# Eleven row gathers of an edge slot issued in rows of three, the later rows held for TensorE's progress (graph convolutions, one core)

## What is computed

```
def conv(h, W, b):
    m = jnp.concatenate([h[dst], h[src], edge_attr], axis=1) @ W + b
    return jax.ops.segment_sum(m, dst, num_segments=n_nodes)
h = jax.nn.relu(conv(x, W1, b1))
h = jax.nn.relu(conv(h, W2, b2))
return conv(h, W3, b3)
```

## Time and profile before

| what | us |
|---|---|
| median of 3 runs | 12742.13 |
| lowest, highest | 12732.27, 12769.19 |
| span of the profiled execution | 13058.8 |
| POOL busy in it | 5588.0 |
| PE busy in it | 8138.5 |
| convolutions 1, 2, 3, roughly | 82 to 2458, 2466 to 4150, 4150 to 5890 |

### The profile page before, as it was taken

The page is one execution under the profiler, slowest core; times in us unless marked ns, Lnnn a source line. Parts: engine busy times, 40 slices in busy tenths (PEclk is TensorE's granted clock), DMA queues, the critical chain, the costliest instruction groups (busy, mean ns, idle before and its releaser), DMA issues. The chain is left out here.

```text
span 13058.8 us, 166557 instructions
## 1 busy us (share of the span) xinstructions
PE 8138.5 (62%) x53406; PEld 6241.7 (48%) x53407; DVE 4466.3 (34%) x5989; ACT 2268.9 (17%) x3783; POOL 5588.0 (43%) x5903
## 2 busy tenths in 40 slices
PE   5676667666666666665565665565655555555565
PEld 3444444455555555554444444444444444444444
DVE  5444444211112111113333333333443333333334
ACT  4444444100000000001111111111111111111112
POOL 3333332444443444443444444444344444444443
PEclk8877888777776776776777777777777777777777
DMA  4333334344445444443111111111111111111111
GB/s 144 143 136 142 138 139 142 133 164 164 164 164 168 165 164 164 164 164 89 42 42 42 45 41 45 42 38 42 42 57 41 42 42 42 44 41 39 42 43 53
DMA packets 409727, 1226.47 MB, mean 94 GB/s; under 512 B 119675, under 2 KB 212947, under 8 KB 360990
## 3 DMA queue, kind: packets, MB, share of 16 engines
q1 hardware_dynamic: 207943, 741.50, 15.8%
q0 software_dynamic: 188528, 235.73, 7.8%
q10 hardware_dynamic: 13160, 248.08, 4.8%
HBM read 943.27 MB, written 281.57 MB: 94 GB/s over the span
## 5 line engine op out<-in xcount | busy, mean ns | idle before, releaser
L2095 POOL DMA_INDIRECT data<-q_rows,idx x3328 | 3159.9, 949 | 3809.6 <-ACT idx L2223 2722.0
L971 POOL DMA_INDIRECT data<-h_parts,idx x2508 | 2382.6, 950 | 3422.0 <-PE p_part L986 2505.3
L1101 PE MATMUL p_z<-hs,adj 128*128 128x192 bf16 x22442 | 2779.3, 276 | 1291.2 <-issue 1277.0
L1101 PEld LDWEIGHTS p_z<-hs,adj 128*128 128x128 bf16 x22442 | 2189.8, 109 | 1981.3 <-issue 1799.9
L2299 DVE TENSOR_TENSOR_SCAN run<-reset,run,p_turn 128x1024 f32<-128x1024 bf16 x416 | 976.3, 2347 | 2841.3 <-DMA nodes<-kept_quads 2407.5
L2126 PE MATMUL part<-hot,back 128*128 128x128 f32 x6688 | 1069.2, 315 | 738.0 <-ACT back L2228 387.1
L2115 PE MATMUL p_back<-ident,run 128*128 128x128 f32 x3344 | 596.9, 338 | 1250.3 <-DVE run L2299 1206.8
L2126 PEld LDWEIGHTS part<-hot,back 128*128 128x128 f32 x6688 | 973.9, 226 | 736.6 <-issue 736.0
L2228 ACT COPY back<-p_back 128x1024 f32<-128x1024 f32 x418 | 423.2, 1012 | 5115.9 <-PE p_back L2115 3092.3
L2115 PEld LDWEIGHTS p_back<-ident,run 128*128 128x128 f32 x3344 | 509.5, 179 | 1632.7 <-issue 1632.6
L2121 PE MATMUL part<-hot,t 128*128 128x128 f32 x6688 | 1036.4, 321 | 254.8 <-issue 254.4
(11 more groups left out here) (363 smaller groups left out, 6537.6 us busy)
## 6 DMA issues: line engine op xcount, KB each, us to landing
adj<-counted SPq DMA_DIRECT2D x304, 1568.0 KB
counted<-adj ACTq DMA_DIRECT2D x76, 3136.0 KB
reset<-flags SPq DMA_DIRECT2D x208, 512.0 KB
data<-q_rows,idx POOLq DMA_INDIRECT x3328
data<-h_parts,idx POOLq DMA_INDIRECT x2508
feat<-in_ea_blocks SPq DMA_DIRECT2D x208, 128.0 KB
ea<-in_ea_cols SPq DMA_DIRECT2D x154, 88.0 KB, 1.9
rden<-node_rows SPq DMA_DIRECT2D x50, 256.0 KB
```

The lines of the kernel that those rows point to most:

```text
L971: pool.indirect_dma_start(out=data[:, p % HELD, j, 0:PARTS], out_offset=None, in_=table[:, :], in_offset=bass.IndirectOffsetOnAxis(ap=idx[ ...
L1101: mm = pe.matmul(p_z[:, 0:PARTS], adj[:, (q + LAG) % 2, hi, :], hs[:, hi, :], start=(hi == 0), stop=(hi == BLOCKS - 1))
L2095: pool.indirect_dma_start(out=data[:, r, j, :], out_offset=None, in_=q_rows[:, :], in_offset=bass.IndirectOffsetOnAxis(ap=idx[:, r, j:j + ...
```

## The change

POOL's eleven gathers of a slot are cut into rows of 3, 3, 3 and 2. The first row goes out as before; ahead of columns 3, 6 and 9 POOL waits for TensorE's progress through the dense group that follows the `by_window` that freed the slot. In convolutions 2 and 3 the marks are the blocks `hi` 32, 64 and 80, for which PE's matmuls get a new semaphore `s_pace`; in convolution 1 they are the ends of count steps 2, 5 and 8 (the semaphore `s_count`, which was there). At the start, slots that have no such dense group yet (`alone`) are gathered without the waits, and for this the first turn of POOL's loop stands outside of it.

```diff
+    PACED = (3, 6, 9)
+    PACES = (32, 64, 80)
...
+        s_pace = sem("s_pace")
...
-            with pool.Fori(0, KT) as k:
+            def paced(k, p, j):
+
+                group = k * NQ + (p + 1 - HELD)
+                if first:
+                    pool.wait_ge(s_count, group * GC + (j + 2))
+                else:
+                    pool.wait_ge(s_pace, group * (len(PACES)) + PACED.index(j) + 1)
+                gate(pool)
+
+            def gather(k, p, pos, alone):
+                pool.wait_ge(s_idx[p], k + 1)
+                pool.wait_ge(s_part, k * H + (H + nth[pos] + 1 - HELD * (H // len(POS_P))))
+                gate(pool)
+                for j in range(GC):
+                    if j in PACED and not alone:
+                        paced(k, p, j)
+                    pool.indirect_dma_start(
+                        out=data[:, p % HELD, j, 0:PARTS], out_offset=None, in_=table[:, :],
+                        in_offset=bass.IndirectOffsetOnAxis(ap=idx[:, p, j:j + 1], axis=0),
+                    ).then_inc(s_row[p], 16)
+
+            for p, pos in enumerate(POS_P):
+                gather(0, p, pos, p + 1 < HELD)
+            with pool.Fori(1, KT) as k:
                 for p, pos in enumerate(POS_P):
-                    pool.wait_ge(s_idx[p], k + 1)
...
+                    gather(k, p, pos, False)
...
+                        if not first and hi in PACES:
+                            mm.then_inc(s_pace, 1)
```

More of the change, by code:

```diff
@@ L964, in _ @@
             further_windows_of(pool, further)
-            with pool.Fori(0, KT) as k:
-                for p, pos in enumerate(POS_P):
-                    pool.wait_ge(s_idx[p], k + 1)
[L968 to L974, removed]
+            def paced(k, p, j):
[19 more added lines that the diff above has]
+            with pool.Fori(1, KT) as k:
+                for p, pos in enumerate(POS_P):
+                    gather(k, p, pos, False)
         @block.tensor
```

## The result

The changed kernel takes 11967.9 us (median of 3 runs, 11958.6 to 11972.0), the kernel before 12742.1: a ratio of 0.939, with a 95% interval of 0.937 to 0.941. The forecast was 11960 us. The profiled run of the changed kernel is its timed run, so here span and time agree.

The account below looks back on a forecast made before the run. No engine was taken as full; POOL's gather bursts were taken to slow TensorE and hold up its semaphores. Convolutions 2 and 3 -433, convolution 1 -395, waits +50 made -778 us: 11960 us, range 11300 to 12850.

Parts of the forecast that it names:

- The cause: In the convolutions, POOL's gather burst slows TensorE after some 55 to 60 pairs and holds its semaphores; 8.7 us a slot.
- Rival 1: Convolutions: the burst is not the cause, nothing gained, only the waits' cost remains; 12790 us, chance 0.07.
- The rule of the Trainium skill: At SBUF, TensorE never waits on anyone, so gathers do not slow PE; no saving, only 50 us of waits.
- Row 1, then row 2: Convolutions 2 and 3: block 32's wait holds nothing, six gathers form one 7.5 us burst, PE slows at 5.0 us.
- Rows 3 and 4: Convolutions 2 and 3: block 64's wait pauses POOL 3.0 us; then five gathers follow directly, 6.25 us.
- Convolutions 2 and 3, the sum: POOL binds with one and a half pauses, 18.25 us a slot against 21.1; 433 us less.
- Convolution 1, the sum: Burst ends 6.0 us earlier, the work behind it stays; 22.5 us a slot, 395 us less.
- The waits: POOL's satisfied waits cost 0.1 us each on the 456 of convolutions 2 and 3; 50 us more.
- The sum: Whole kernel: -433 - 395 + 50 = -778 us; 11964 us against the median, stated as 11960.
- Rival 2: At the group's boundary, rows 3 and 4 hold PE's semaphores until row 4 ends; slower, 13150 us, chance 0.13.
- Rival 3: Convolutions: more gained, one pause a slot at 16.75 us, convolution 1 at 18.5 us; 11380 us, chance 0.2.
- What would show it: Trace signs: gathers in six and five, 17 to 20 and 20 to 24 us slots, PE's "issue" time about halved.

Follow-up runs that it names:

- g_timed: The change, but in convolutions 2 and 3 one 1700-element memset between third and fourth gather replaces the waits; 12020.5 us, 0.920 of the kernel before.
- g_timed2: The change, but in convolutions 2 and 3 one 700-element memset between third and fourth gather replaces the waits; 11878.3 us, 0.928 of the kernel before (chip B).
- e_before: The kernel before, unchanged, run again for a second trace; 13087.9 us, ratio 1.000, profiled span 13097 us.
- c_onewait: The change, but in convolutions 2 and 3 only the wait for block 32 is kept; 12132.9 us, 0.928 of the kernel before.
- r_after: The change, unchanged, run beside the kernel before on one chip; 12114.9 us, 0.926 of the kernel before.
- d_sixfive: The change, but in convolutions 2 and 3 only the waits for blocks 64 and 80 are kept; 11983.6 us, 0.915 of the kernel before.
- j_both: The change without block 32's wait in convolutions 2 and 3, plus four memsets between PNA's fourth and fifth gathers; 11507.4 us, 0.879 of the kernel before.

## Why the prediction was right, and where not

- **The cause.** Right: the bursts of gathers slow TensorE and hold its updates. Rival 1 (nothing gained) is out; breaking the bursts with no wait on PE at all, and with PE's instructions as before in convolutions 2 and 3, gives the gain (`g_timed`, `g_timed2`), so PE's own program alone is not it, nor is the recording (`e_before`). Nor does a fetch of PE's code show: in the trace before, the two queues that bring instructions have no packet between 2478 and 4119 us, while the stall is in every slot there. The rule of the Trainium skill, "SBUF — State Buffer", section "SBUF: two separate sides", by which nothing should be saved, does not cover what happens here: its sentence is on SBUF's ports, and what is late here is PE's issue and its updates. No run here says at which place they meet.
- **Row 1, then row 2.** Wrong. "This wait holds nothing and six gathers still form one burst" was the step that failed. With the change PE starts its group together with row 1, and its first 17 blocks take 0.164 us each, not 0.083, at a granted clock of 0.50 behind a stand of 6 us, so POOL waits 1.80 us for block 32. `c_onewait` shows that this wait alone carries 326 of the 359 us in convolutions 2 and 3.
- **Rows 3 and 4.** Wrong as to place: rows 2 to 4 are mostly one burst of eight, not six and five. The wait for block 64 finds it done (the gather behind it comes 1.25 us after the one before, as without a wait); that for block 80 adds something in 34 of 146 slots (69 in `r_after`).
- **Convolutions 2 and 3, the sum.** The forecast was 18.25 us a slot without the finished nodes' work, 2.85 us less than before, and -433 us. With that work in it the mean slot went from 22.8 and 23.0 us to 20.2 and 20.5, some 2.5 us less; trace to trace that is 380 us, on one chip 365. The number came out nearly, for another reason: the slot is now 3 gathers, the wait, 8 gathers and then some 2 us until the held updates arrive, not 11 gathers and one and a half pauses. The forecast's own geometry, built in `d_sixfive`, saves more than was forecast for it: 3640 to 3126 us, 514 us.
- **Convolution 1, the sum.** Right in kind, mis-sized: 5.2 us a slot were forecast, -395 us; measured 8.0 us at the mean (28.1 to 20.1) and -609 us, on one chip -581. This is the term of the sum that was most off. The forecast kept the 10.7 us behind the burst as they were and took only the end of the burst forward; with rows apart the stall itself is about 3 us (PE stands from 1209.38 to 1212.44 in the slot above) and the granted clock goes to 0.96.
- **The waits.** +50 us were taken for 0.1 us each. In front of columns 6 and 9 they can be read from the spacing of the gathers, 1.25 us where there is no wait (`c_onewait`): 0.16 us a slot more in the trace after, 0.35 in `r_after`, 24 and 54 us in all. They did not slow the kernel, as `c_onewait` without them is 33 us slower in these stages. That `g_timed` without waits in convolutions 2 and 3 is 79 us faster than `r_after` there is the break's place and length as much as the waits.
- **The sum.** -778 us was forecast against -774 measured between the two medians. That agreement is luck in part, since the same terms stand against 989 us in the three convolutions from trace to trace, and on one chip the change saves 968 us (13083 to 12115), and the convolutions' stages 949. On record the kernel before is 12742 us with a profiled span of 13059, 317 us more, of which the prediction left open how much was the recording's; `e_before` shows none of it, so that profile and those times are of different chips or sessions. PNA passes without a cut are 6944 to 6959 us in the trace after and on chip B and 7039 to 7112 elsewhere, a part of the difference. Why the kernel before differs by 2.4 to 2.7% between chips and the change by 1.2% is open.
- **Two checks in the prediction.** The top of "11600 to 12600 us" does not follow from its own terms: two pauses in every slot and half the gain in convolution 1 give 12742 - 205 - 198 + 50 = 12389 us. And 3.1 MB do not fit into 18 us at the 165 GB/s of the earlier trace rows, which move 2.97 MB; the changed kernel moves 182 to 184 GB/s in these stages, at a DMA share of 0.53, so nothing came of it.
- **Rival 2.** Its mechanism came true: the boundary's updates are held until the burst ends, `zs` 6.8 us late at the median, PE idle 6.0 us. By the prediction's last paragraph, semaphores late at the boundary were a sign of its being wrong, and that sign is there. Its price did not, as it added this stop to the stall inside the group, and that stall is gone. It was listed as the way to a slower kernel; here it is a cost inside a faster one. That it is what limits the change is argued from `d_sixfive`, which has a prompt boundary and is faster, but has other bursts too.
- **Rival 3.** Not reached in convolutions 2 and 3; convolution 1 came near its 18.5 us (19.0 at the median, 20.1 at the mean).
- **What would show it.** Right: 17 to 20 us a slot at the median in convolutions 2 and 3; 20.1 in convolution 1 at the mean, at the edge of its 20 to 24 (19.0 at the median, below it); clock above before; SP's late waits down by a third (966.1 us in 1550, 419.4 in 1000). Wrong: two runs of six and five; the new wait in the third row; PE's "issue" fell to a tenth, not by half; POOL's new waits stand in front of row 2.

## What to carry to other kernels

When an engine crawls with no partner in the waits, or its consumers stand for "remote" long after it is done, look at what POOL's indirect gathers do in that stretch, and cut the run of gathers; a cut on a timer worked as well here as one tied to TensorE's progress, which moves a burst as easily as it cuts it, so count the burst lengths in the new trace. Then look for the same pattern in the stages that the idea was not made for: in PNA one cut gave 1300 us, more than the change itself.

## What the runs showed of the hardware

- TensorE's updates are held beside a run of indirect gathers even when TensorE is not slowed: 6.8 us at the median in convolutions 2 and 3 of the change, 6.6 us in the PNA slot shown. In these convolutions they mostly arrive 1.3 to 1.7 us behind the end of the last gather (93% of 152 are over 1 us late); in PNA some arrive while gathers still go out (6023.28 in `j_both`).
- What a pause is worth depends on what runs around it: between four and four of PNA's gathers 2.1 us more than the usual spacing bring the copies that are over 3 us late from 33% to 11%, and 1.1 us leave them at 30%; in the convolutions 0.56 us behind three gathers give TensorE 19 more blocks.
- Four gathers a slot still leave gaps of 0.35 to 0.61 us behind the 59th or 64th block of a group (64th at the median), so a short burst does not prevent them; with the change's pause behind three gathers PE runs all 98 blocks. Where gathers and TensorE meet, and why near 60 pairs, stays open.
